# A ViT tower on one core: attention normalised in the transposed domain, and a new order of the engines

## The reference, cut to what matters

```python
h = tok(x) @ W + b                       # 128 images, 196 patches of 16x16 with four shifted copies, D = 192
h = concat([cls_tok, h])                 # 197 tokens
xn = layernorm(h)
q, k, v = heads(xn @ Wq.T), heads(xn @ Wk.T), heads(xn @ Wv.T)      # 6 heads of 32
scores = q @ k.T * 32**-0.5 + (lam * (q @ anchor_h))[..., None]
h = h + (softmax(scores) @ v) @ Wo.T
y = layernorm(h)
y = clip(round(y / 0.02), -128, 127).int8 @ weight_t                # exact integer sums
h = h + y * (0.02 * 0.01) + bias
```

## Time and profile before

| | us |
|---|---|
| three runs | 1737.76, 1737.85, 1738.62 (median 1737.85) |
| span of the profiled execution | 1736.1 |
| VectorE busy in it | 1471.9 |
| ScalarE busy in it | 759.4 |
| GpSimd busy in it | 925.9 |

### The profile page before, as it was taken

One profiled execution on the slowest core, in us unless ns is written; L12 is line 12 of the kernel. 1 busy time (PEld: TensorE's weight loads), 2 busy tenths in 40 slices (PEclk: granted clock), 3 DMA queues, 4 the chain that ended last, 5 costly groups with the idle time before them and its releaser, 6 DMA issues.

```text
span 1736.1 us, 53274 instructions
## 1 busy us (share of the span) xinstructions
PE 1655.0 (95%) x16368; PEld 1504.7 (87%) x16368; DVE 1471.9 (85%) x3906; ACT 759.4 (44%) x1751; POOL 925.9 (53%) x1911
## 2 busy tenths in 40 slices
PE   4999999996699999999999999999999999999996
PEld 4999999996588888888888888888888888888884
DVE  7888888895388988888888888888888888888885
ACT  2000000001265555556565555655556555555653
POOL 3353544536055655555555565556555555555555
PEclk9999999998699999999999999999999999999998
DMA  9999999973777778787887878877787878878771
GB/s 299 265 306 297 314 290 308 314 257 143 123 140 151 142 146 146 148 147 138 148 149 149 145 139 147 150 146 143 143 147 146 150 138 147 147 150 145 139 119 33
DMA packets 216158, 303.66 MB, mean 175 GB/s; under 512 B 47776, under 2 KB 205011, under 8 KB 205988
## 3 DMA queue, kind: packets, MB, share of 16 engines
q1 hardware_dynamic: 204690, 227.17, 65.4%
q10 hardware_dynamic: 7426, 39.47, 7.8%
q0 software_dynamic: 3984, 36.28, 5.3%
HBM read 126.54 MB, written 58.29 MB: 106 GB/s over the span
## 4 chain that ended last, share of the span: by engine, by line
PE 50%; DVE 8%; POOL 7%; issue 7%; DMA 2%; SPq 1%; ACT 0%; ACTq 0%; POOLq 0%; DVEq 0%
PE bank L874 9%; PE o_bank L932 8%; PE bank L922 6%; PE bank L908 6%; PE bank L895 5%; PE bank L883 5%; PE o_bank L855 3%; PE o_bank L951 2%; PE bank L855 2%; PE o_bank L960 2%; POOL ln L163 2%; DVE neg_max L1193 2%; PE bank L1007 2%; DMA k_st<-qk_lo 2%; POOL qx L1369 2%
## 5 line engine op out<-in xcount | busy, mean ns | idle before, releaser
L1093 ACT ACTIVATE probs<-bank 99x396 f32<-99x396 f32 x768 | 381.8, 497 | 217.7 <-PE bank L922 217.4
L1336 POOL TENSOR_TENSOR key_sum<-probs 99x396 f32<-99x396 f32 x256 | 227.4, 888 | 433.5 <-ACT probs L1093 284.5
L1193 DVE TENSOR_REDUCE neg_max<-bank 99x2 f32<-99x394 f32 x768 | 419.4, 560 | 16.4 <-PE bank L908 12.3
L340 PE MATMUL bank<-e_t,xt 128*128 128x192 f32 x2352 | 389.0, 329 | 25.2 <-DVE xt L448 21.5
L340 PEld LDWEIGHTS bank<-e_t,xt 128*128 128x128 f32 x2352 | 387.5, 192 | 26.4 <-DVE xt L448 26.2
L922 PE MATMUL bank<-q_st,k_st 99*99 99x198 f32 x1536 | 280.6, 264 | 5.7 <-DMA q_st<-max_rows 2.9
L908 PE MATMUL bank<-k_st,q_st 96*99 96x198 f32 x1536 | 275.6, 275 | 10.1 <-DMA k_st<-qk_lo 4.1
L448 DVE STREAM_TRANSPOSE xt<-x_t 128x256 f32<-128x256 f32 x588 | 214.9, 416 | 46.0 <-PE bank L340 44.6
L922 PEld LDWEIGHTS bank<-q_st,k_st 99*99 99x99 f32 x1536 | 208.0, 167 | 50.5 <-issue 42.5
L908 PEld LDWEIGHTS bank<-k_st,q_st 96*99 96x99 f32 x1536 | 193.3, 167 | 26.8 <-issue 12.6
L932 PE MATMUL o_bank<-probs,vals 99*32 99x198 f32 (+1 forms) x3072 | 199.0, 337 | 0.0
(11 more groups left out here) (134 smaller groups left out, 3593.0 us busy)
## 6 DMA issues: line engine op xcount, KB each, us to landing
x_t<-in_x_dram SPq DMA_DIRECT2D x26, 1344.0 KB, 21.9
x_t<-in_x_dram ACTq DMA_DIRECT2D x26, 1344.0 KB, 23.1
q_st<-qk_hi SPq DMA_DIRECT2D x126, 198.0 KB, 4.4
k_st<-qk_hi SPq DMA_DIRECT2D x126, 198.0 KB, 4.4
xn_in<-xn_scratch SPq DMA_DIRECT2D x128, 148.5 KB
h_in<-h_scratch SPq DMA_DIRECT2D x128, 148.5 KB
h_scratch<-h_t POOLq DMA_DIRECT2D x13, 1344.0 KB, 17.2
xn_scratch<-xn_t POOLq DMA_DIRECT2D x13, 1344.0 KB, 8.0
```

Of the source, the lines that this page charges most:

```text
L340: last = pe.matmul(token_bank(p)[:, 0:D], xt[:, p, c // 3, c % 3, :], e_t[:, row_kind(t), col, c // 3, c % 3, :], start=c == 0, stop=c == 5)
L1093: nc.scalar.activation(probs[:, n.two, h, :, :], wide(T_BANK, TC), ACT.Exp).then_inc(exp_done, 1)
L1193: nc.vector.tensor_reduce(out=neg_max[:, n.two, :, h], in_=wide(S_BANK[h % 2], TC)[:, :, 0:NTOK], axis=AX_X, op=ALU.max, negate=True).then ...
L1336: nc.gpsimd.tensor_tensor(key_sum[:, b.two, heads, :], probs[:, b.two, heads, 0, :], probs[:, b.two, heads, 1, :], ALU.add).then_inc(pool_ ...
```

## The change

`build_attention` is changed, with the two banks that the token stage uses (now 2 and 3) and the host's order of the output weights (heads now in plain order).

The normalising no longer turns anything. TensorE spreads each head's sum over 32 rows, the same rows as the head's values, with a `ones` weight of 32 columns: for heads 0 to 3 from `key_sum` into the second bank of `o_bank`, for heads 4 and 5 straight from `probs`, beside their values. ScalarE takes the logarithm of the sums (two instructions) and then exp(-log), `near`, a near reciprocal. VectorE forms `unity` = sum x near and `rough` = values x near, and `att_t` = (unity - 2) x rough, one step of Newton's method with the sign turned; h1 subtracts the projected rows in place of adding them. ScalarE's high part and the low parts are taken from `att_t` in SBUF, one of the low parts by GpSimd (`a_lo`). `o_t`, `turn_back`, the reciprocal, `att` and its turning, and VectorE's share of `key_sum` are gone. ScalarE loads the table set that has both functions, once, ahead of the loop.

The maxima are taken two heads at a time, from a pair of banks. `attend` is cut into `attend_first` (heads 0 to 3) and `attend_rest` (heads 4, 5 and all sums). The maxima are turned into a MISC bank.

The order of every engine's step is new. The FFN (g) is now that of i-4, with the turning in the same step; the layer norm and quantising are one step later (q = i-3); the value projection is that of b; heads 4 and 5 of the exponentials are in the step of c; the last step is B+4 in place of B+3. SyncE sends the first q blocks before it loads xn, and their low part last in the odd step. GpSimd's step is now: the layer norm chain of q, key sums of heads 2 and 3 of c, qx of q, `a_lo` of e, key sums of heads 0 and 1 of b, `hb` of e.

The diff, cut to what the steps below speak of (the orders stand above):

```diff
-        banks = [ctx.enter_context(nc.psum_tensor(f"bank{i}", [128, 512], F32)) for i in range(6)]
+        banks = [ctx.enter_context(nc.psum_tensor(f"bank{i}", [128, 512], F32)) for i in range(4)]
+        s_pair = ctx.enter_context(nc.psum_tensor("s_pair", [128, 2, 512], F32))
-    key_sum = tile("key_sum", [TC, NS, H, TP])
-    o_t = tile("o_t", [TILE, NS, 2, TP])
-    inv_sum = tile("inv_sum", [TC, NS, 2, H])
-    att = tile("att", [TC, NS, 2, D])
+    key_sum = tile("key_sum", [TC, NS, SIDE, TP])
+    log_sum = tile("log_sum", [DA, 2, TP])
+    near = tile("near", [DA, 2, TP])
+    unity = tile("unity", [DA, 2, TP])
+    rough = tile("rough", [DA, 2, TP])
+    att_t = tile("att_t", [DA, 2, TP])
-    S_BANK, T_BANK, MISC = banks[0:2], banks[2], banks[3:6]
+    T_BANK, MISC = banks[0], banks[1:4]
+    O_ROWS, SUM_ROWS = o_bank[:, 0, :], o_bank[:, 1, :]
-        for i in range(last, B + 4):
+        for i in range(last, B + 5):
         # SyncE, step
+                if usual and odd:
+                    sp.wait_ge(qkhi_done, p.pair_count(3, 1))
+                    stack(p, q_st, 0, q_first, qk_hi[:, 0, :])
+                    stack(p, q_st, 1, q_first, qk_hi[:, 0, :])
...
+                if usual and odd:
+                    sp.wait_ge(qklo_done, p.pair_count(3, 1))
+                    stack(p, q_st, 2, q_first, qk_lo[:, 0, :])
         # TensorE
-                if n.reuses(1) or h >= 2:
-                    pe.wait_ge(max_done, n.count(H, h - 1))
+                if h % 2 == 0 and (n.reuses(1) or h >= 2):
+                    pe.wait_ge(max_done, n.count(HG, h // 2))
                 for c in range(2):
-                    last = pe.matmul(S_BANK[h % 2][0:TC, c * TP:(c + 1) * TP],
+                    last = pe.matmul(s_pair[0:TC, h % 2, c * TP:(c + 1) * TP],
...
-            def attend(n):
-
-                def add_values(at, col, kc):
-                    h = HEAD_AT[at]
+            def add_values(n, h, kc):
+                kk = TC if kc == 0 else NTOK - TC
+                at, cols = (h, FIRST) if h < SIDE else (h - SIDE, REST)
+                pe.matmul(O_ROWS[at * HD:(at + 1) * HD, cols], vals[0:kk, n.two, kc, h, :],
+                          probs[0:kk, n.two, h, kc, :], start=kc == 0, stop=kc == 1)
+
+            def attend_first(n):
+
+                pe.wait_ge(exp_done, n.count(H, SIDE))
+                pe.wait_ge(v_done, n.count(1, 1))
+                if n.reuses(1):
+                    pe.wait_ge(rough_done, n.count(1, 0))
+                for kc in range(2):
+                    for h in range(SIDE):
+                        add_values(n, h, kc)
+
+            def attend_rest(n):
+
+                pe.wait_ge(exp_done, n.count(H, H))
+                for kc in range(2):
                     kk = TC if kc == 0 else NTOK - TC
-                    pe.matmul(o_bank[at % 4 * HD:(at % 4 + 1) * HD, 0, col:col + TP], vals[0:kk, n.two, kc, h, :],
-                              probs[0:kk, n.two, h, kc, :], start=kc == 0, stop=kc == 1)
-
-                pe.wait_ge(exp_done, n.count(H, H - 1))
-                pe.wait_ge(v_done, n.count(1, 1))
-                for kc in range(2):
-                    for at in range(4):
-                        add_values(at, 0, kc)
-                for j in range(HG):
-                    if j == 0:
-                        pe.wait_ge(exp_done, n.count(H, H))
-                        pe.wait_ge(pool_sums, n.count(2, 2))
-                    if j < 2:
-                        for at in (4, 5):
-                            add_values(at, TP, j)
-                    else:
-                        pe.wait_ge(dve_sums, n.count(1, 1))
-                    for side in range(2):
-                        to = (2 + side) * HD
-                        last = pe.matmul(o_bank[to:to + HD, 0, TP:2 * TP], pick[:, j, :],
-                                         key_sum[:, n.two, HEAD_AT[side * HG + j], :], start=j == 0, stop=j == HG - 1)
+                    for h in range(SIDE, H):
+                        add_values(n, h, kc)
+                    for h in range(SIDE, H):
+                        to = (h - SIDE + 2) * HD
+                        last = pe.matmul(O_ROWS[to:to + HD, REST], ones[0:kk, :], probs[0:kk, n.two, h, kc, :],
+                                         start=kc == 0, stop=kc == 1)
                 last.then_inc(av_done, 1)
-
-            def turn_back(n):
-
-                pe.wait_ge(ot_done, n.count(1, 1))
-                for c in range(2):
-                    for t in range(2):
-                        last = pe.transpose(o_bank[0:TC, 1, (2 * c + t) * TILE:(2 * c + t + 1) * TILE],
-                                            o_t[:, n.two, t, c * TC:(c + 1) * TC], ident[:, :])
-                last.then_inc(back_done, 1)
+                pe.wait_ge(pool_sums, n.count(2, 2))
+                if n.reuses(1):
+                    pe.wait_ge(unity_done, n.count(1, 0))
+                for h in range(SIDE):
+                    last = pe.matmul(SUM_ROWS[h * HD:(h + 1) * HD, FIRST], ones[:], key_sum[:, n.two, h, :],
+                                     start=True, stop=True)
+                last.then_inc(sums_done, 1)
...
         # ScalarE, step
+                if has_e:
+                    act.wait_ge(att_done, e.count(1, 1))
+                    if e.reuses(NS):
+                        act.wait_ge(op_done, e.count(1, 1 - NS))
+                    copy(a_mix[:, e.two, :, :], att_t[:], ahi_done)
...
+                if has_c:
+                    act.wait_ge(av_done, c.count(1, 1))
+                    nc.scalar.activation(log_sum[0:DB, 1, :], O_ROWS[DB:DA, REST], ACT.Ln).then_inc(log_done, 1)
+                    act.wait_ge(sums_done, c.count(1, 1))
+                    nc.scalar.activation(log_sum[:, 0, :], SUM_ROWS[:, FIRST], ACT.Ln).then_inc(log_done, 1)
...
+                    act.wait_ge(log_done, c.count(2, 2))
+                    nc.scalar.activation(near[:], log_sum[:], ACT.Exp, scale=-1.0).then_inc(near_done, 1)
...
+            nc.scalar.preload_act_table_set("natural_log_exp_and_others")
         # VectorE
+            def maxima(n, j):
+                dve.wait_ge(scored, n.count(H, 2 * j + 2))
+                if j == 0 and n.reuses(NS):
                     dve.wait_ge(mpart_done, n.count(2, 2 - 2 * NS))
-                nc.vector.tensor_reduce(out=neg_max[:, n.two, :, h], in_=wide(S_BANK[h % 2], TC)[:, :, 0:NTOK],
+                both = s_pair[0:TC, :, 0:2 * TP].rearrange("p h (c n) -> p h c n", c=2)[:, :, :, 0:NTOK]
+                nc.vector.tensor_reduce(out=neg_max[:, n.two, :, 2 * j:2 * j + 2].rearrange("p c h -> p h c"), in_=both,
                                         axis=AX_X, op=ALU.max, negate=True).then_inc(max_done, 1)
...
+                if has_e:
+                    nc.vector.tensor_tensor(unity[:, 0, :], SUM_ROWS[:, FIRST], near[:, 0, :],
+                                            ALU.mult).then_inc(unity_done, 1)
...
+                    dve.wait_ge(unity_done, e.count(1, 1))
+                    dve.wait_ge(rough_done, e.count(1, 1))
+                    if e.reuses(1):
+                        dve.wait_ge(pool_lo, e.count(1, 0))
+                        dve.wait_ge(alo_done, e.count(1, 0))
+                    nc.vector.scalar_tensor_tensor(out=att_t[:], in0=unity[:], scalar=2.0, in1=rough[:],
+                                                   op0=ALU.subtract, op1=ALU.mult).then_inc(att_done, 1)
...
+                    nc.vector.tensor_tensor(a_mix[DB:DA, e.two, 1, :], att_t[0:DB, 1, :],
+                                            a_mix[0:DB, e.two, 1, :].bitcast(F32), ALU.subtract).then_inc(alo_done, 1)
...
+                    nc.vector.tensor_tensor(h1[:, e.two, :, :], h_in[:, e.two, :, :], rows(MISC[0]),
+                                            ALU.subtract).then_inc(h1_done, 1)
+                if has_c:
+
+                    dve.wait_ge(near_done, c.count(1, 1))
+                    nc.vector.tensor_tensor(unity[0:DB, 1, :], O_ROWS[DB:DA, REST], near[0:DB, 1, :], ALU.mult)
...
+                    nc.vector.tensor_tensor(rough[:], wide(O_ROWS, DA), near[:], ALU.mult).then_inc(rough_done, 1)
         # GpSimd, step
+                    nc.gpsimd.tensor_tensor(a_lo[:, e.two, :], att_t[:, 0, :], a_mix[:, e.two, 0, :].bitcast(F32),
+                                            ALU.subtract).then_inc(pool_lo, 1)
```

More of the change, by code:

```diff
@@ L248, in token_bank @@
     def token_bank(p):
-        return banks[4 + p]
+        return banks[2 + p]
     def load_row(eng, t, quarters):
@@ L640, in build_attention @@
     ST = 3 * HD
-    TILE = 4 * HD
+    SIDE = 4
     SPLIT = H - 4
@@ L659, in build_attention @@
     vals = tile("vals", [TC, NS, 2, H, HD])
-    pick = tile("pick", [TC, HG, HD])
+    ones = tile("ones", [TC, HD])
     neg_max = tile("neg_max", [TC, NS, 2, H])
@@ L1219, in step @@
                     maxima(a, 0)
-                    maxima(a, 1)
-                if has_c and not (has_p and not odd):
```

(1 more changed line is left out.)

430 lines of the change are left out of this document (185 added, 245 removed).

## The result

The changed kernel takes 1744.73 us (median of 8 runs, 1739.48 to 1750.17); the kernel before takes 1737.8 on the same chips (8 runs, 1734.34 to 1739.69). The ratio is 1.0041, 95% interval 1.0025 to 1.0057: slower by 0.4%, where 1677 was forecast. The time lies 29 us above the end of the range. The profiled execution took 1741.97 with a span of 1740.2.

What follows compares the result with a forecast made beforehand. TensorE's stream was taken as the bound, VectorE second. Stream 9.04, loop turn 0.08 and waits 0.15 make 9.27 us a step against 9.78; 64 us saved, 3 added at the end: 1677 us, range 1643 to 1716.

Steps and rivals of the forecast that it cites:

- SyncE and DMA: Load queue: last k stack of an even step keeps 0.9 us of slack; moving the odd step's low q stack costs nothing.
- Rival 4: A cost on VectorE or in a stack's landing of over 0.5 us a step eats all: 1738 and above, chance 0.09.
- VectorE's work stays what it is: VectorE: 1.70 us removed, 1.83 added, maxima save 0.1; about 8.3 in an even step, 8.6 in an odd one.
- Rival 2: VectorE's loop binds: 0.5 us longer than reckoned, it adds 0.25 a step, 32 us more: 1709, chance 0.18.
- the walk: VectorE's loop from output projection to second maximum, 4.8 us, against TensorE's 5.3 in an even step: 0.5 to spare.
- GpSimd's step: GpSimd's busy time per step: 5.2 to 5.4 us becomes 5.8 of 8.57, with a_lo added at about 0.45.
- TensorE's stream: TensorE's matmuls per step: 0.84 us removed, 0.34 added for a second 32-column visit; even 8.57, odd 9.50, mean 9.04.
- rival 1: TensorE's second 32-column visit is cheap or the waits vanish: 25 us less, 1652, chance 0.14.
- The ends: Pipeline's end, one step longer: bounded by 0 and one step, taken as 3 us.
- ScalarE and the table: ScalarE: at most 1.0 us net more a step, with 2 to spare; new table load ahead of the loop costs nothing.
- Rival 3: ScalarE's logarithm and exponential evict each other's table: two loads, 2.57 us a step, 1967 in all, chance 0.03.

Runs made afterwards that it cites:

- light sums: Changed kernel with GpSimd's two key sums cut to 8 of 198 columns, the rest of the sums held constant: 1721.8 us, ratio 0.9924.
- h_in early: Changed kernel with SyncE issuing the load of h_in first in its step, ahead of the stacks and xn: 1709.34 us, ratio 0.9846.
- h_in and guard: Changed kernel with h_in loaded first and GpSimd's key sum of heads 0 and 1 waiting for both parts of the maxima: 1687.54 us, ratio 0.9723.

## Why the prediction was wrong, point by point

**SyncE and DMA ("nothing") failed.** The step followed the stacks past which the loads were moved, and not the landing of h_in itself: issued 4.7 into its step, landed 5.0 later, used 9.7 in. 0.31 a step of direct wait; its removal is worth 34 us. The earlier trace rows had a landing time of 5.2 for a stack in the same queue, which was enough to see it. Rival 4 named the place ("a stack's landing"), at 0.09.

**VectorE ("VectorE's work stays what it is") failed.** By instructions it holds: the maximum took 974 ns for 1.0, `att_t` 561 for 0.57. What was not counted is when they run: cast +0.44 and quantising +0.10 (458 ns, 356 before), together 0.54 a step, in 9.07 busy where 8.3 to 8.6 was said. With light sums the rows shrink back, to 8.50 a step (799.09 / 94). That 8.50 lies in the range is partly luck: the six steps of the earlier trace rows give 8.72 before, more than the two steps that were read, and the maxima save 0.34 a step (300.9 to 269.8 us in 92 steps), not 0.1. The wait of 76.6 us on `max_parts` was read in the earlier trace rows and not asked about. The Trainium skill's rule (SBUF — State Buffer, Who interferes with whom) bears on this change and was not weighed. Rival 2 saw VectorE's loop as the bound for its length, and its sign, TensorE waiting for the maxima, is in the trace. But both rows go with h_in early, where VectorE's instructions are as long as before: it became late for the load and the holds. In the walk TensorE's terms add up to 5.14, not 5.3, so the spare was 0.34; it was enough.

**GpSimd's step** was put at 5.8; it is 6.81 (40.84 / 6). Its step before was read low, 5.2 to 5.4, where six steps of the earlier trace rows give 5.79 (34.73 / 6). `a_lo` takes 664 ns for 0.45, and never under 600 in the 30 from 1000 to 1300 us, so most of that is its own length. The key sums are held, 1214 for 888, twice a step. And `a_lo`, which was given no price on TensorE, is late in every second step:
```profile
1115.69 0.43 PE L925 MATMUL bank<-q_st,k_st 99*99 99x198 f32 x2
1116.40 0.30 PE L898 MATMUL bank<-wo_hi,a_mix 128*99 128x192 f32 x1 [0.28 <-POOL a_lo L1338]
```
That is 0.71 from start to start, where the steps without the wait take 0.27: about 0.2 a step, still there with h_in and guard. That its layer norm chain stops holding VectorE's qx was right: that wait, is not among those after.

**TensorE's stream was right.** Both visits of the 32-column mode show, the second for the first time. Timeline of TensorE after, start and duration:
```profile
1102.68 0.35 PE L877 MATMUL bank<-x_lo,wb_rest 97*128 97x396 f32 x1
...
1102.96 0.88 PE L933 MATMUL o_bank<-probs,vals 99*32 99x198 f32 x16
...
1103.77 0.43 PE L925 MATMUL bank<-q_st,k_st 99*99 99x198 f32 x2
...
1104.04 0.49 PE L1024 MATMUL bank<-ffn_w_bf,qx_t 96*99 96x192 bf16 x4
...
1105.03 0.40 PE L925 MATMUL bank<-q_st,k_st 99*99 99x198 f32 x2
...
1105.37 0.36 PE L933 MATMUL o_bank<-probs,vals 99*32 99x198 f32 x2
...
1106.51 0.43 PE L925 MATMUL bank<-q_st,k_st 99*99 99x198 f32 x2
```
The first visit takes 0.81 for four rounds of 0.165 (0.66), with 0.10 before it (0.28 from start to start in place of 0.18) and 0.08 behind: 0.33. The second takes 1.14 for six rounds (0.99), with 0.09 before it (0.34 from start to start, where the earlier trace rows have 0.25 for a score behind transposes) and 0.08 behind: about 0.33 again. The drain that the Trainium skill states (TensorEngine Tiling (Array Packing), Key Properties) is paid twice, as was taken; rival 1's cheap second visit is out. With h_in and guard the odd step is 9.59 (stream forecast 9.50), the mean 9.31 (forecast 9.27).

**The ends were too cheap.** With h_in and guard the span is 1685.8. 125 steps at 9.78 less 9.315 save 58 us, and 1736.1 less 58 is 1678: the ends cost 8, not 3 (10, if the 1735.4 of the kernel before beside it is taken). The first result comes at 504.7 in place of 502.3; the start of the pipeline, one step longer, was left out.

**ScalarE and the table were right.** Logarithms 337 and 332 ns, exponential from SBUF 527. Rival 3's evictions don't occur: the trace after has two table loads in all, the second ahead of the loop.

In sum: 9.27 was forecast, 9.80 measured, and 0.49 of the 0.53 between them goes when h_in is early and the guard is back.

## What to carry to other kernels

When a step is moved in a queue, write down for each transfer in it the time of issue, of landing and of use, those that move along too. A wait on an engine that is half idle may keep it out of another one's way: before it is dropped, look which SBUF instructions of VectorE and GpSimd it keeps apart. In this kernel an instruction whose mean grew though its shape stayed was waiting inside, and moving it handed part of the wait to the next one.

## What the runs showed of the hardware

- A cast of 99x12 from 174 to 610 ns in the mean, up to 0.75 us, and a subtraction of 99x12 from 172 to 794, both ending when GpSimd's instruction does.
- It goes both ways: GpSimd's key sum of 396 columns from 888 to 1214 ns in the mean, and 1.42 to 1.80 us where `att_t` follows; two columns from 194 ns to 1.28 us. Here the hold is longer than `att_t`'s 0.56: the GpSimd instruction starts inside the maximum ahead of `att_t` and ends 0.05 (two columns) or 0.75 us (396 columns) after `att_t`.
- VectorE's maxima, which read PSUM, were not lengthened: 974 ns in the mean after, 0.97 to 0.98 in the 92 from 1000 to 1300 us. Neither were its bn_stats beside `hb`, 343 ns.
- A maximum over 788 columns of two banks, 974 ns, costs less than two of 394 (560 each), but put into the kernel before it costs 64 us.
- Each pass of 32-column products between full-width ones costs 0.33 us beyond its rounds.
